# Dilation on one core: seven row sides as relu chains merged half by half into pair tiles, more clamped GpSimd pairs, other tile pitches and orders

## The chip, the core and the metric

The kernel runs on one core of a Trainium2 chip. Its time is device microseconds of that core. The core has TensorE (PE in the profile), VectorE (DVE), ScalarE (ACT), GpSimd (POOL) and SyncE (SP), which run their own instruction streams and meet at semaphores, 16 DMA engines, SBUF and PSUM as on-chip memory. GpSimd has no access to PSUM in this kernel: what lies in PSUM is touched by TensorE, ScalarE and VectorE alone.

## The reference, cut to what matters

`x` is (8, 32, 256, 256) in float32. It is normalised by groups of two channels, dilated with an 11 x 11 kernel for each channel and added to itself; then a second stage (projection, 3 x 3 depthwise convolution, batch norm, gelu, a small offset, bilinear resampling) is added too.

```python
def dilation(u, kernel, r):                       # r = 5, ks = 11, NEG = -1e30
    pad = jnp.pad(u, ((0, 0), (0, 0), (r, r), (r, r)), constant_values=NEG)
    kflat = kernel.reshape(C, ks * ks)
    def body(acc, idx):
        di = idx // ks
        dj = idx % ks
        sl = jax.lax.dynamic_slice(pad, (0, 0, di, dj), (Bn, C, H, W))
        return jnp.maximum(acc, sl - kflat[:, idx][None, :, None, None]), None
...
x = x + _L0_conv_ref(_gn(x), L0_conv_finsler_params)      # the dilation: 121 taps
x = x + _L1_conv_ref(_gn(x), ...)                         # convolution and resampling
```

## The kernel before, in words

The 256 planes lie in two groups of 128 partitions. A plane of 256 rows is taken in 16 windows of 16 rows (`WR`), each as two chunks of 8 rows (`CR`): 64 chunks, each 128 partitions x 2048 elements. `stats_and_tables` runs first, then `dilation` (L334 to L718), `convolution` and `resample`.

A window `u` has rows padded to `UC` = 266 elements; `dx` (`difference`, L179) holds u shifted by one minus u. The maximum of two neighbouring taps is base + relu(difference + gap), so a pair of taps costs one relu step, one addition of u and one maximum. There are three ways to do it:

- GpSimd pairs ("m", tiles `m`, 4 of them): ScalarE writes the relu (`pair_relu`, order letter r) or GpSimd itself a clamp of dx (`clamp`, L488, letter c, for pairs in `CLAMPED`); GpSimd adds u (`pair`, L496 and L500, letter t); VectorE takes the maximum into `acc_a` (L688, letter m).
- DMA pairs ("y", tiles `t`, 4): ScalarE writes the relu (letter x), GpSimd issues an accumulating DMA of u onto it (`add_u`, L471, letter i), VectorE merges it (letter y).
- Chains: one side of a kernel row, 5 or 6 taps, as repeated relu in PSUM, in two halves of 4 rows (`chain[0]`, `chain[1]`, letters 0 and 1): ScalarE a relu (`chain_step`, L609), TensorE adds dx or at last u (L559). VectorE merges the finished half into `acc_b` in SBUF (`merge_chain`, L662). The next chain's first relu waits for that (`chain_taken`).

Single taps (letter s) go from u into acc_a at once. `acc_a` lies in PSUM, each instruction on it waits for the one before (`a_done`). ScalarE starts acc_b from one tap (`start_b`, L576, letter b). At a chunk's end `join` takes the maximum of acc_a and acc_b (L695) and writes x1 = acc_a x rstd + u (L701), which SP stores; ScalarE squares x1 for the next statistics (letter u, L583), and the x1 of the next chunk waits for that. GpSimd also makes dx for the next window in pieces (L181, letter d).

Each engine's order inside a chunk is written out by hand in the strings `ACT_ORDER`, `PE_ORDER`, `DVE_ORDER`, `POOL_ORDER`. Counts per chunk, before: ScalarE 16 r, 16 x, 58 chain halves, b, u; VectorE 22 m, 16 y, 9 s, 12 chain merges, join, x1; GpSimd 22 t, 16 i, 6 c, 2 d; TensorE 58 half steps. A tile is free when VectorE has merged the pair that used it 4 pairs earlier (`a_free`, L404).

In `resample` (L1279 ff.) GpSimd makes three differences of y for each of 64 steps: dh (L1288, inputs one element apart), dv (L1291, inputs one row apart, y has pitch 257) and dd (L1295); VectorE does ten steps of 1024 elements with them.

## Time and profile before

| | |
|---|---|
| median of 3 runs | 10327.33 us (10327.08 to 10329.48) |
| profiled execution | 10330.04 us, span 10328.2 us |
| mean granted TensorE clock | 0.965 |
| VectorE, GpSimd, ScalarE, TensorE busy | 97%, 91%, 89%, 83% |
| t transfers (accumulating DMA) | 1024, 1059 KB each |

Busy shares are over the whole span and mix four stages. An instruction's duration on GpSimd reaches into the next one's; where an engine is never idle, the distance from start to start is what an instruction costs. The last part of the page, the chain that ended last, lies in the resampling alone and tells nothing of the dilation.

### The profile page before, as it was taken

The numbers are of one execution on the slowest core, as the hardware profiler recorded it, in microseconds if no ns is written. First come the engines' busy times: TensorE is split into PE (matmuls) and PEld (weight loads), VectorE is DVE, ScalarE is ACT, GpSimd is POOL, SyncE is SP. The second block draws the span as 40 slices with busy tenths as digits, with TensorE's granted clock in tenths as the row PEclk, the third lists the DMA queues.
The fourth block names the chain that finished last, engine by engine and source line by source line (L and its number), as shares of the span: only waits on it lengthen the run. The fifth ranks groups of instructions, "written<-read, shape, count | busy, mean of one in ns | idle before, by whom it ended". The sixth has DMA issues, their size and how long they took to land. (4 is left out here: it accounts for less than half of the span.)

```text
span 10328.2 us, 72612 instructions
## 1 busy us (share of the span) xinstructions
PE 8605.7 (83%) x18068; PEld 3331.9 (32%) x18068; DVE 9972.2 (97%) x5624; ACT 9184.8 (89%) x6857; POOL 9430.7 (91%) x3274
## 2 busy tenths in 40 slices
PE   2888888888888888888888888888888887997998
PEld 0333333333333333333333333333333332443333
DVE  8999999999999999999999999999999998999999
ACT  2999999999999999999999999999999997888776
POOL 2999999999999999999999999999999996777999
PEclk9999999999999999999999999999999998999999
DMA  8888878888888888788888888888888876444776
GB/s 320 152 155 154 153 153 156 159 158 157 157 157 158 157 158 160 150 158 160 157 157 157 156 156 156 159 157 159 157 158 157 157 139 132 173 189 178 264 278 253
DMA packets 442070, 1751.41 MB, mean 170 GB/s; under 512 B 23889, under 2 KB 130385, under 8 KB 392785
## 3 DMA queue, kind: packets, MB, share of 16 engines
q0 software_dynamic: 278528, 1110.51, 60.5%
q1 hardware_dynamic: 163152, 636.41, 16.3%
q8 instruction: 159, 2.61, 0.1%
q14 instruction: 231, 1.88, 0.1%
HBM read 391.58 MB, written 201.33 MB: 57 GB/s over the span
## 5 line engine op out<-in xcount | busy, mean ns | idle before, releaser
L559 PE MATMUL chain<-dx,mats 128*128 128x512 f32 x10240 | 5007.4, 635 | 922.9 <-ACT chain L609 921.4
L500 POOL TENSOR_TENSOR m<-m,u 128x2048 f32<-128x2048 f32 x1024 | 4817.0, 4891 | 25.0 <-ACT m L591 23.9
L688 DVE SCALAR_TENSOR_TENSOR acc_a<-m,kt,acc_a 128x2048 f32<-128x2048 f32 x1344 | 3162.9, 2353 | 74.0 <-POOL m L500 22.7
L559 PEld LDWEIGHTS chain<-dx,mats 128*128 128x128 f32 x10240 | 1923.6, 197 | 4006.5 <-ACT chain L609 2089.1
L609 ACT ACTIVATE chain<-chain,gap_r 128x1024 f32<-128x1024 f32 x2560 | 2699.5, 1089 | 233.7 <-PE chain L559 231.6
L688 DVE SCALAR_TENSOR_TENSOR acc_a<-t,kt,acc_a 128x2048 f32<-128x2048 f32 x1024 | 2412.0, 2355 | 34.2
L471 POOL DMA_DIRECT2D t<-u x1024 | 1680.5, 1752 | 396.8 <-ACT t L591 335.5
L496 POOL TENSOR_TENSOR m<-u,m 128x2048 f32<-128x2048 f32 x384 | 1914.8, 4986 | 0.0
L591 ACT ACTIVATE t<-dx,gap_l 128x2048 f32<-128x2048 f32 x768 | 1541.6, 2007 | 0.7 <-DVE acc_a L688 0.7
L559 PE MATMUL chain<-u,mats 128*128 128x512 f32 x3072 | 1456.0, 605 | 74.0 <-ACT chain L609 74.0
L688 DVE SCALAR_TENSOR_TENSOR acc_a<-u,kt,acc_a 128x2048 f32<-128x2048 f32 x576 | 1357.1, 2356 | 20.5
L591 ACT ACTIVATE m<-dx,gap_l 128x2048 f32<-128x2048 f32 x640 | 1282.3, 2004 | 22.6 <-DVE acc_a L688 22.6
L662 DVE SCALAR_TENSOR_TENSOR acc_b<-chain,kt,acc_b 128x1024 f32<-128x1024 f32 x768 | 966.6, 1279 | 69.6 <-PE chain L559 69.0
L559 PE MATMUL chain<-dx,neg_ident 128*128 128x512 f32 x1536 | 744.4, 621 | 330.9 <-ACT chain L609 313.6
L488 POOL TENSOR_SCALAR m<-dx,gap_l 128x2048 f32<-128x2048 f32 x384 | 989.4, 2577 | 12.8 <-DVE acc_a L688 12.6
L609 ACT ACTIVATE chain<-dx,gap_r 128x1024 f32<-128x1024 f32 x640 | 713.2, 1122 | 241.7 <-DVE acc_b L662 228.6
L559 PEld LDWEIGHTS chain<-u,mats 128*128 128x128 f32 x3072 | 547.2, 188 | 952.1 <-issue 557.7
L591 ACT ACTIVATE m<-dx,gap_r 128x2048 f32<-128x2048 f32 x384 | 766.8, 1997 | 0.0
L1052 DVE SCALAR_TENSOR_TENSOR hp<-o,par,hp 128x1024 f32<-128x1024 f32 x512 | 623.8, 1295 | 19.7 <-PE hp L863 19.6
L559 PEld LDWEIGHTS chain<-dx,neg_ident 128*128 128x128 f32 x1536 | 274.6, 192 | 800.7 <-ACT chain L609 520.8
L591 ACT ACTIVATE t<-dx,gap_r 128x2048 f32<-128x2048 f32 x256 | 516.7, 2018 | 13.9 <-PE chain L542 13.9
L964 POOL TENSOR_TENSOR tap_a<-tap_a,tap_b 128x2048 f32<-128x2048 f32 x64 | 291.7, 4558 | 236.8 <-ACT tap_b L927 225.8
(144 smaller groups left out, 7133.1 us busy)
## 6 DMA issues: line engine op xcount, KB each, us to landing
t<-u POOLq DMA_DIRECT2D x1024, 1059.0 KB, 8.8
u<-x_dram SPq DMA_DIRECT2D x32, 2688.0 KB, 30.8
xw<-x_scratch SPq DMA_DIRECT2D x62, 1152.0 KB, 7.3
xt<-x_dram SPq DMA_DIRECT2D x32, 2048.0 KB, 14.4
x_scratch<-x SPq DMA_DIRECT2D x64, 1024.0 KB, 10.6
h_scratch<-h SPq DMA_DIRECT2D x32, 2048.0 KB, 7.2
hw<-h_scratch SPq DMA_DIRECT2D x64, 1024.0 KB, 9.3
out_dram<-res SPq DMA_DIRECT2D x64, 1024.0 KB, 4.9
```

Source lines behind the costliest of these rows:

```text
L471: nc.gpsimd.dma_start(t[j % TP][:].rearrange("p r w -> p (r w)")[:, 0:RUN], u[s][:].rearrange("p r w -> p (r w)")[:, first:first + RUN], a ...
L488: nc.gpsimd.tensor_scalar(m[j % MP], dx[s][:, top:top + CR, lo:lo + W], high, low, ALU.min, ALU.max).then_inc(m_clamped, 1)
L496: nc.gpsimd.tensor_tensor(m[j % MP], rows, m[j % MP], ALU.add if outer > base else ALU.subtract).then_inc(m_ready, 1)
L500: nc.gpsimd.tensor_tensor(m[j % MP], m[j % MP], rows, ALU.add).then_inc(m_ready, 1)
L559: added = nc.tensor.matmul(chain[h][:, r:r + 2, :], weight, src[:, top:top + 2, dj:dj + W], start=False, stop=True, skip_group_check=True)
L591: return nc.scalar.activation(dst, dx[s][:, k * CR + di:k * CR + di + CR, lo:lo + W], ACT.Relu, bias=gap[:, g, col(di, base):col(di, base) ...
L609: nc.scalar.activation(chain[h][:], src, ACT.Relu, bias=gap[:, g, col(di, base):col(di, base) + 1], scale=scale).then_inc(chain_relu[h], 1)
L662: nc.vector.scalar_tensor_tensor(out=part, in0=chain[h][:], scalar=kt[:, g, base:base + 1], in1=part, op0=ALU.subtract, op1=ALU.max).then_ ...
L688: nc.vector.scalar_tensor_tensor(out=acc_a[:], in0=src, scalar=k_base, in1=acc_a[:], op0=ALU.subtract, op1=ALU.max).then_inc(a_done, 1)
L964: nc.gpsimd.tensor_tensor(tap_a[n % 2][:, rows, :], tap_a[n % 2][:, rows, :], tap_b[:, rows, :], ALU.add).then_inc(pool_adds, 1)
L1052: nc.vector.scalar_tensor_tensor(out=out, in0=o[n % 3][:, q * QR + ty:(q + 1) * QR + ty, tx:tx + W], scalar=par[:, COL_DW + t:COL_DW + t + 1],
```

## The change

- `CHAINS` gets a third entry (links) and a seventh chain: rows 0 (left) to 5 with 4 links (5 taps), row 6 with 5 links (6 taps). Before, six chains, the right ones with 5 links. The number of chain halves on ScalarE and TensorE stays 58.
- Pairs: 22 on GpSimd, 18 by DMA (16 before), 5 singles (9 and the one of acc_b before). Ten GpSimd pairs are clamped (6 before), so ScalarE has 12 r and 18 x.
- `acc_b`, `start_b` and the maximum in `join` are gone. A finished chain half is merged into a half of a pair tile that is ready but not yet merged (`chain_targets`: the second m or y tile that follows in `DVE_ORDER`), with the difference of the two kernel values (`k_gap`, 28 one-column subtractions ahead of the loop) as scalar. It waits for that tile (`tile_ready`), and the tile's own merge waits for the chain half (`chain_taken`).
- Five m and five t tiles instead of four each. The m tiles have pitch 266 instead of 260, and a pair's view starts at column (di * 266 + base + 2) % 4.
- y in `resample` has pitch 258 instead of 257.
- All four orders are new; VectorE's first instruction of a chunk is a single, the square moves to the end of ScalarE's chunk.
- The program is built with `dynamic_dma_scratch_size=4096`, the space for descriptors of the DMAs that GpSimd issues.

```diff
--- before.py
+++ after.py
@@ -48,20 +48,17 @@
-CHAINS = ((0, "left"), (1, "right"), (2, "right"), (3, "right"), (4, "right"), (5, "right"))
-NPOOL, NDMA = 16, 16
-CLAMPED = (1, 5, 9, 12, 16, 20)
-MP, TP = 4, 4
-ACT_ORDER = "x0x01r01xr10b1r01r01x01x01r01xr0u10r10x10x10x1r01r01r01x01x01x01r01r01x01r01rx010r10x10r10x1"
-PE_ORDER = "0011010101010101010101010101010101010101010101010101010101"
-DVE_ORDER = "m01mmymysss0m1myysymmy01mmsmyyms01msymsymm01ymymyysm0m1mymy"
-POOL_ORDER = "iitcitttcitittittcitdititcittiicttditittictitt"
+CHAINS = ((0, "left", 4), (1, "right", 4), (2, "right", 4), (3, "right", 4), (4, "right", 4), (5, "right", 4), (6, "right", 5))
+NPOOL, NDMA = 22, 18
+CLAMPED = (0, 2, 3, 4, 7, 8, 11, 12, 13, 15)
+MP, TP = 5, 5
+ACT_ORDER = "x0x10r10x10x1x0r10r10x10x1r01x01x01x01r0101x01r1x0x1x01x01r01x0r10r10r1010rx01x01r01u0101"
+PE_ORDER = "0101010101010101010101010101101010101010101010100101010101"
+DVE_ORDER = "smy0m1ymymms01myymym01mymymy1y0mmmyms10ymysym10mmymmyym01sy"
+POOL_ORDER = "cdcdcititticitttciitictitcittcitictitticitittttiitit"
@@ -74,20 +71,35 @@
     pairs, singles = [], []
+    sides = {di: (side, links) for di, side, links in CHAINS}
     for di in range(KS):
-        side = dict(CHAINS).get(di)
+        side, links = sides.get(di, (None, 0))
...
             pairs += [(di, 1, 0), (di, 3, 2)]
-            singles += [(di, 4)]
+            if links == 4:
+                pairs += [(di, 5, 4)]
+            else:
+                singles += [(di, 4)]
...
             singles += [(di, 10)]
-    while len(pairs) > NPOOL + len(CLAMPED) + NDMA:
+    while len(pairs) > NPOOL + NDMA:
...
+def chain_targets():
+    targets = {}
+    order = list(numbered(DVE_ORDER))
+    for place, (kind, ch) in enumerate(order):
+        if kind in "01":
+            tiles = [x for x in order[place + 1:] if x[0] in "my"]
+            targets[int(kind), ch] = tiles[:2][-1]
+    return targets
@@ -336,8 +348,9 @@
     D_TURNS = POOL_ORDER.count("d")
-    pool_pairs, dma_pairs, (init_b, *singles) = dilation_taps()
-    NPAIR = NPOOL + len(CLAMPED)
+    pool_pairs, dma_pairs, singles = dilation_taps()
+    targets = chain_targets()
+    NPAIR = NPOOL
@@ -352,8 +365,8 @@
     chain_steps = []
-    for ch, (di, side) in enumerate(CHAINS):
-        bases = range(1, 5) if side == "left" else range(9, 4, -1)
+    for ch, (di, side, links) in enumerate(CHAINS):
+        bases = range(1, 1 + links) if side == "left" else range(9, 9 - links, -1)
@@ -371,9 +384,9 @@
-        m = [sb(f"m{s}", [P, CR, W + 4])[:, :, 0:W] for s in range(MP)]
+        m_tiles = [sb(f"m{s}", [P, CR, UC]) for s in range(MP)]
         t = [sb(f"t{s}", [P, CR, UC]) for s in range(TP)]
-        acc_b = sb("acc_b", [P, CR, W])
+        k_gap = sb("k_gap", [P, GROUPS, 2 * NCHAIN])
@@ -392,11 +405,23 @@
         chain_taken = [sem(f"chain_taken{h}") for h in range(2)]
-        b_started = sem("b_started")
+        k_gap_ready = sem("k_gap_ready")
         a_done = sem("a_done")
-        merged = sem("merged")
...
+        def m_tile(j):
+            di, base, outer = pool_pairs[j]
+            first = (di * UC + base + 2) % 4
+            return m_tiles[j % MP][:, :, first:first + W]
+        def tile_of(kind, j):
+            return m_tile(j) if kind == "m" else t[j % TP][:, :, 0:W]
+        def tile_col(kind, j):
+            di, base, outer = pool_pairs[j] if kind == "m" else dma_pairs[j]
+            return col(di, outer if kind == "m" and j in CLAMPED else base)
@@ -485,7 +510,7 @@
                     passed(pool, pool_turns)
-                    nc.gpsimd.tensor_scalar(m[j % MP], dx[s][:, top:top + CR, lo:lo + W], high, low,
+                    nc.gpsimd.tensor_scalar(m_tile(j), dx[s][:, top:top + CR, lo:lo + W], high, low,
@@ -493,11 +518,11 @@
                         pool.wait_ge(m_clamped, c * len(CLAMPED) + (CLAMPED.index(j) + 1))
-                        nc.gpsimd.tensor_tensor(m[j % MP], rows, m[j % MP],
+                        nc.gpsimd.tensor_tensor(m_tile(j), rows, m_tile(j),
...
                         pool.wait_ge(m_begun, c * NRELU + (relu_pairs.index(j) + 1))
-                        nc.gpsimd.tensor_tensor(m[j % MP], m[j % MP], rows, ALU.add).then_inc(m_ready, 1)
+                        nc.gpsimd.tensor_tensor(m_tile(j), m_tile(j), rows, ALU.add).then_inc(m_ready, 1)
@@ -545,7 +570,7 @@
                     ch, step, base = chain_steps[i]
-                    di, side = CHAINS[ch]
+                    di, side, _ = CHAINS[ch]
@@ -569,13 +594,6 @@
             def _(act):
-                def start_b(c, s, k):
-                    di, dj = init_b
-                    act.wait_ge(merged, at(c, 1, 0))
-                    nc.scalar.activation(acc_b[:], u[s][:, k * CR + di:k * CR + di + CR, dj:dj + W], ACT.Identity,
-                                         bias=nkt[:, g, col(di, dj):col(di, dj) + 1]).then_inc(b_started, 1)
@@ -594,7 +612,7 @@
                     ch, step, base = chain_steps[i]
-                    di, side = CHAINS[ch]
+                    di, side, _ = CHAINS[ch]
@@ -626,14 +644,12 @@
                                         act.wait_ge(a_done, a_free(c, "m", relu_pairs[j], NPAIR, MP))
-                                        pair_relu(s, k, pool_pairs[relu_pairs[j]], m[relu_pairs[j] % MP]) \
+                                        pair_relu(s, k, pool_pairs[relu_pairs[j]], m_tile(relu_pairs[j])) \
...
                                         pair_relu(s, k, dma_pairs[j], t[j % TP][:, :, 0:W]).then_inc(t_ready, 1)
-                                    elif kind == "b":
-                                        start_b(c, s, k)
@@ -644,59 +660,61 @@
                 nc.vector.memset(x1[:], 0.0).then_inc(pads_set, 1)
+                for g in range(GROUPS):
+                    for (h, ch), tile in targets.items():
+                        last = col(CHAINS[ch][0], chain_steps[last_step[ch]][2])
+                        other = tile_col(*tile)
+                        nc.vector.tensor_tensor(k_gap[:, g, 2 * ch + h:2 * ch + h + 1], kt[:, g, last:last + 1],
+                                                kt[:, g, other:other + 1], ALU.subtract).then_inc(k_gap_ready, 1)
+                dve.wait_ge(k_gap_ready, GROUPS * 2 * NCHAIN)
                 dve.sem_inc(a_done, NA)
-                dve.sem_inc(merged, 1)
...
-                def merge_chain(c, h, ch):
-                    di, side = CHAINS[ch]
-                    base = col(di, chain_steps[last_step[ch]][2])
-                    part = acc_b[:, h * HR:(h + 1) * HR, :]
-                    dve.wait_ge(chain_added[h], c * NSTEP + (last_step[ch] + 1))
-                    dve.wait_ge(chain_taken[h], at(c, NCHAIN, ch))
-                    if ch == 0:
-                        dve.wait_ge(b_started, c + 1)
-                    nc.vector.scalar_tensor_tensor(out=part, in0=chain[h][:], scalar=kt[:, g, base:base + 1], in1=part,
-                                                   op0=ALU.subtract, op1=ALU.max).then_inc(chain_taken[h], 1)
-                def merge(c, s, k, kind, j):
+                def tile_ready(c, kind, j):
...
                         dve.wait_ge(m_ready, c * NPAIR + (j + 1))
-                        di, base, outer = pool_pairs[j]
-                        if j in CLAMPED:
-                            base = outer
-                        src = m[j % MP]
-                    elif kind == "y":
+                    else:
                         dve.wait_ge(t_added[j % TP], c * (len(range(j % TP, NDMA, TP)) * 16) + (j // TP + 1) * 16)
-                        passed(dve, dve_turns)
-                        di, base, outer = dma_pairs[j]
-                        src = t[j % TP][:, :, 0:W]
+                def merge_chain(c, h, ch):
+                    tile = targets[h, ch]
+                    part = tile_of(*tile)[:, h * HR:(h + 1) * HR, :]
+                    dve.wait_ge(chain_added[h], c * NSTEP + (last_step[ch] + 1))
+                    tile_ready(c, *tile)
+                    if ch > 0 and targets[h, ch - 1] == tile:
+                        dve.wait_ge(chain_taken[h], at(c, NCHAIN, ch))
+                    nc.vector.scalar_tensor_tensor(out=part, in0=chain[h][:],
+                                                   scalar=k_gap[:, g, 2 * ch + h:2 * ch + h + 1], in1=part,
+                                                   op0=ALU.subtract, op1=ALU.max).then_inc(chain_taken[h], 1)
+                def merge(c, s, k, kind, j):
+                    if kind == "s":
+                        di, base = singles[j]
+                        src, at_col = u[s][:, k * CR + di:k * CR + di + CR, base:base + W], col(di, base)
                     else:
-                        di, base = singles[j]
-                        src = u[s][:, k * CR + di:k * CR + di + CR, base:base + W]
-                    k_base = kt[:, g, col(di, base):col(di, base) + 1]
+                        tile_ready(c, kind, j)
+                        src, at_col = tile_of(kind, j), tile_col(kind, j)
+                        for h in range(2):
+                            taken = [ch for (half, ch), tile in targets.items() if half == h and tile == (kind, j)]
+                            if taken:
+                                dve.wait_ge(chain_taken[h], at(c, NCHAIN, max(taken) + 1))
+                    k_base = kt[:, g, at_col:at_col + 1]
...
                         dve.wait_ge(joined, at(c, 1, 0))
-                        passed(dve, dve_turns)
...
-                def join(c, s, k):
+                def finish(c, s, k):
+                    dve.wait_ge(x1_squared, c + 1)
                     dve.wait_ge(a_done, at(c, NA, NA))
-                    for h in range(2):
-                        dve.wait_ge(chain_taken[h], at(c, NCHAIN, NCHAIN))
-                    nc.vector.tensor_tensor(acc_a[:], acc_a[:], acc_b[:], ALU.max).then_inc(merged, 1)
-                    dve.wait_ge(x1_squared, c + 1)
-                    dve.wait_ge(merged, at(c, 1, 1))
-                    passed(dve, dve_turns)
@@ -715,7 +733,7 @@
                                         merge(c, s, k, kind, j)
-                                join(c, s, k)
+                                finish(c, s, k)
@@ -1074,7 +1092,7 @@
         xw = [sb(f"xw{s}", [P, VR + 1, W]) for s in range(XS)]
-        y = [sb(f"y{s}", [P, VR + 1, W + 1]) for s in range(2)]
+        y = [sb(f"y{s}", [P, VR + 1, W + 2])[:, :, 0:W + 1] for s in range(2)]
@@ -1440,7 +1458,8 @@
     }
-    nc = bacc.Bacc("TRN2", target_bir_lowering=False, num_devices=1)
+    nc = bacc.Bacc("TRN2", target_bir_lowering=False, num_devices=1,
+                   dynamic_dma_scratch_size=4096)
...
     build(nc, *args, out)

```

## Rows read from the trace of the kernel before

**Rows 1.** The profile page, part 1: busy us of each engine and its share.
```profile
PE 8605.7 (83%) x18068; PEld 3331.9 (32%) x18068; DVE 9972.2 (97%) x5624; ACT 9184.8 (89%) x6857; POOL 9430.7 (91%) x3274
```

**Rows 2.** The trace by line, L685, the first VectorE instruction of each of 64 chunks.
```profile
L685 DVE TENSOR_SCALAR acc_a<-m,kt x64: 2353/2354/2356, 212.8 to 8588.3; 128x2048 f32<-128x2048 f32 x64
```

**Rows 3.** The timeline of VectorE, one chunk's end: start us, us, instruction, idle before.
```profile
3001.92 2.36 DVE L688 SCALAR_TENSOR_TENSOR acc_a<-m,kt,acc_a 128x2048 f32<-128x2048 f32 x1
3004.31 2.36 DVE L688 SCALAR_TENSOR_TENSOR acc_a<-t,kt,acc_a 128x2048 f32<-128x2048 f32 x1
3006.86 2.30 DVE L695 TENSOR_TENSOR acc_a<-acc_a,acc_b 128x2048 f32<-128x2048 f32 x1 [0.20 <-DVE acc_a L688]
3009.40 2.35 DVE L701 SCALAR_TENSOR_TENSOR x<-acc_a,small,u 128x2048 f32<-128x2048 f32 x1 [0.24 <-DVE acc_a L695]
3011.90 2.35 DVE L685 TENSOR_SCALAR acc_a<-m,kt 128x2048 f32<-128x2048 f32 x1
3014.17 2.47 DVE L662 SCALAR_TENSOR_TENSOR acc_b<-chain,kt,acc_b 128x1024 f32<-128x1024 f32 x2
3016.55 2.35 DVE L688 SCALAR_TENSOR_TENSOR acc_a<-m,kt,acc_a 128x2048 f32<-128x2048 f32 x1
```

**Rows 4.** The timeline of GpSimd in the dilation.
```profile
3006.34 3.35 POOL L488 TENSOR_SCALAR m<-dx,gap_l 128x2048 f32<-128x2048 f32 x1
3008.26 2.60 POOL L471 DMA_DIRECT2D t<-u  x1
...
3029.49 2.33 POOL L471 DMA_DIRECT2D t<-u  x1
3030.28 5.76 POOL L496 TENSOR_TENSOR m<-u,m 128x2048 f32<-128x2048 f32 x1
3034.43 5.75 POOL L500 TENSOR_TENSOR m<-m,u 128x2048 f32<-128x2048 f32 x1
3038.55 2.81 POOL L471 DMA_DIRECT2D t<-u  x1
...
3055.88 3.06 POOL L181 TENSOR_TENSOR dx<-u 128x1060 f32<-128x1060 f32 x1
3057.77 2.32 POOL L471 DMA_DIRECT2D t<-u  x1
```

**Rows 5.** The timeline of ScalarE in the dilation.
```profile
3025.51 2.00 ACT L591 ACTIVATE t<-dx,gap_l 128x2048 f32<-128x2048 f32 x1
3027.40 2.09 ACT L609 ACTIVATE chain<-chain,gap_r 128x1024 f32<-128x1024 f32 x2
3029.39 2.02 ACT L591 ACTIVATE m<-dx,gap_r 128x2048 f32<-128x2048 f32 x1
```

**Rows 6.** DMA view, 1000 to 8000 us: queue's packets, MB, share; issue's KB, us to landing.
```profile
q0 software_dynamic: 229216, 913.88, 73.5%
q1 hardware_dynamic: 102096, 183.01, 7.4%
...
t<-u POOLq DMA_DIRECT2D x844, 1059.0 KB, 8.8
```

**Rows 7.** The timeline of GpSimd in the convolution.
```profile
8976.06 4.55 POOL L969 TENSOR_TENSOR h<-h,tap_a 128x2048 f32<-128x2048 f32 x1
8980.57 4.55 POOL L964 TENSOR_TENSOR tap_a<-tap_a,tap_b 128x2048 f32<-128x2048 f32 x1
```

**Rows 8.** The timeline of GpSimd in the resampling.
```profile
9851.82 4.56 POOL L1291 TENSOR_TENSOR dv<-y 128x2048 f32<-128x2048 f32 x1
9856.45 3.60 POOL L1295 TENSOR_TENSOR dd<-dv 128x2048 f32<-128x2048 f32 x1
9860.01 3.60 POOL L1288 TENSOR_TENSOR dh<-y 128x2048 f32<-128x2048 f32 x1
9863.57 4.55 POOL L1291 TENSOR_TENSOR dv<-y 128x2048 f32<-128x2048 f32 x1
```

**Rows 9.** The timeline of VectorE in the resampling.
```profile
9860.18 1.23 DVE L1371 SCALAR_TENSOR_TENSOR tx<-tx,dd 128x1024 f32<-128x1024 f32 x1 [0.18 <-POOL dd L1295]
```

6 lines of the change are left out of this document (3 added, 3 removed).

## The prediction

> **What bounds the kernel now.** I read the page's busy times first [rows 1]: VectorE is busy for 97% of the span, GpSimd for 91%, ScalarE for 89%, so none of them can be called the bound from that line. The dilation has to be read for itself. Its chunk loop starts 64 times, from 212.8 to 8588.3 us [rows 2]: 8375.5 / 63 = 132.94 us a chunk, 64 chunks are 8508 us, 82% of the span. For what an instruction costs I take the distance to the next start on its engine, not its duration, because on GpSimd the durations overlap: a pair addition is shown with 5.75 us, yet the next instruction starts 4.12 us later [rows 4].
>
> VectorE, by its timeline [rows 3]: a maximum into acc_a 2.39 us when another follows, 2.27 when a chain merge follows, 2.55 at the end of the chunk, a chain merge 1.19 (two in 2.38), the join 2.54, the x1 step 2.50. The order of before has 47 instructions into acc_a, 8 of them ahead of a group of chain merges: 38 x 2.39 + 8 x 2.27 + 2.55 + 12 x 1.19 + 2.54 + 2.50 = 130.9 us. That leaves 132.94 - 130.9 = 2.0 us of stalls. GpSimd [rows 4]: 22 pairs x 4.14 (the rows show 4.15 and 4.12), 6 clamps x 1.92, 16 issues x 0.79, two pieces of dx x 1.89: 91.1 + 11.5 + 12.6 + 3.8 = 119.0 us. ScalarE [rows 5]: 32 pair steps x 1.89, 29 x 1.99 for two chain halves, the square and acc_b at least another two at 1.89: 60.5 + 57.7 + 3.8 = 122.0 us. The DMA engines [rows 6]: 73.5% + 7.4% of 132.94 = 97.7 + 9.8 = 107.5 us, or 6.11 us for each of the 16 t transfers. So VectorE is the bound of the dilation, by some 9 us over ScalarE, 12 over GpSimd and 23 over DMA. The resampling stage is the other place touched. There GpSimd runs without a gap, 11.75 us a step (3.56 dh, 4.63 dv with its handover, 3.56 dd) [rows 8], and VectorE waits only 0.18 us of it, for dd [rows 9].
>
> **The change, part by part, in one chunk.** Of 121 taps, seven chains now take 36, 40 pairs take 80, 5 are singles.
>
> VectorE: two y more and four s less (init_b counted out) make 45 instructions into acc_a, the join is gone, and there are 14 chain merges in 9 groups: 35 x 2.39 + 9 x 2.27 + 2.55 + 14 x 1.19 + 2.50 = 125.8 us, 5.1 less. A chain merge into a tile has the shape of one into acc_b, one operand in PSUM and one in SBUF, so I leave it at 1.19. What it adds is a wait: it needs the tile up to two tiles ahead of its own turn, and everything later on VectorE is queued behind it, as are ScalarE's next chain (chain_taken) and the buffers (a_done). Ahead of it only a tile's lateness counts, up to two instructions (4.8 us) earlier than now; the fifth m and t tile give one more buffer for it. A merge directly behind its own chain merge occurs nowhere, there is always an instruction between, so I put no stall there. The 28 one-column subtractions for k_gap stand once ahead of the loop: under 0.1 us each, 2.5 us in all, nothing hides them.
>
> ScalarE: four r less, two x more, no acc_b: 3 x 1.89 less, 116.3 us. The square moves from the first half of the chunk to its end; four chain halves (4 us) are behind it, and x1 is only written again at the next chunk end, so nothing.
>
> DMA: 18 x 6.11 + 9.8 = 119.8 us. This was 23 us clear of VectorE and is now 6 us clear.
>
> GpSimd: four clamps and two issues more, 7.7 + 1.6 us; at the old price of a pair 91.1 + 19.2 + 14.2 + 3.8 = 128.3 us. That is over VectorE's 125.8, so the price of a pair decides. The m tiles get the row pitch of u (266 instead of 260 elements) and a first column that puts every row two elements (8 bytes) off the row of u in its 16 bytes. What do rows say of that? Three forms of one size of addition stand in this trace: dh and dd, whose inputs are one element apart in one tile, 3.56 us; dv and the two additions of the convolution, 4.51 (start to start of h and tap_a [rows 7]; dv took 4.55) [rows 8]; the pairs 4.14. h and tap_a have their rows at the same place in 16 bytes; dv's inputs are 257 elements apart, one element off. In the pairs of before, pitches 260 and 266 differ by 6, so the offset alternates by two elements from row to row: half of the rows of an even base lie as in h, half two elements off. If only the offset within 16 bytes counts, 4.14 is the mean of 4.51 and the price of the other half, which is 2 x 4.14 - 4.51 = 3.77 us. The lower end is 3.56, the upper 4.14 for a price that hangs on something else, and 4.51 if the like pitches put all rows into the slow case. I take 3.77, as the one value that accounts for 4.14 and 4.51 together. GpSimd is then at 82.9 + 19.2 + 14.2 + 3.8 = 120.1 us.
>
> A page speaks against this. The Trainium skill, GPSIMD Engine Reference, section 3 (Performance versus the Vector engine), holds that an addition with two inputs costs about 2.5 to 2.6 cycles an element because both reads go through one port, and gives 4497 ns for 2048 elements; by that there is nothing to gain. This trace agrees for h and tap_a (4.51) and disagrees for dh and dd, the same size at 3.56 to 3.60. By the page all pairs would go at 4.5; what that would make is rival C, worked out there from rows.
>
> So the floor falls from 130.9 to 125.8 us. Stalls were 2.0 us with three engines well clear; now GpSimd and DMA stand at 95% of the floor and ScalarE at 93%. One place is tight: the new chunk begins on GpSimd with clamp, piece, clamp, piece, clamp (9.5 us) ahead of its first issue, and a transfer lands 8.8 us after its issue [rows 6]. The clamp can start only when m20 is merged, 17 us before VectorE ends the chunk (y15, y16, m21, two merges, s4, y17, x1), so the first transfer lands 1.5 us into the next chunk and the second, 6.1 us later, at 7.6, where the first chain merge wants it at 7.05. It just fits, with the x1 store in the same queues. I take 2.8 us of stalls (the old 2.0 and this), 128.6 us a chunk: 64 x (132.94 - 128.6) = 278 us saved. In the resampling y gets pitch 258: dv's inputs are two elements off, the same 3.77; GpSimd needs 11.0 us a step, VectorE's 11.57 becomes the bound, 0.18 x 62 = 11 us. Sum: 278 + 11 - 2.5 = 286.5 us. The profiled execution took 10330.0 us (span 10328.2), the median of the runs is 10327.3, 2.7 lower; from that median 10041 us.
>
> **The rivals.** (A) As told, 10041; by stalls of 1.7 to 4 us, 9971 to 10118.
> (B) The pair stays at 4.14 us. For it: two pairs of different base cost 4.15 and 4.12 [rows 4], as they would if the offset didn't matter. GpSimd is the bound at 128.3; with 2 us of stalls 130.3, with 4 at the chunk's turn, where it waits for m20, 132.3. 64 x (132.94 - 130.3) = 169, and nothing in the resampling: 10161, up to 10290.
> (C) Slower: like pitches put each row into the case of h and dv. 22 x 4.51 + 37.2 = 136.4 us on GpSimd, with 1 us of stalls 137.4: 64 x 4.46 + 2.5 = 288 us more, 10615. It decides from a pair price of (132.9 - 37.2 - 1) / 22 = 4.30 us on; below that the kernel is faster. Against it: only the rows in h's position should cost that, and none is there.
> (D) Pairs at 3.77, but the chunk is held by t transfers: the queue is empty for about 5 us at each chunk's turn (last landing 10 us before the end, where the last chains merge into y17; first bytes of the next 8.8 - 6.1 = 2.7 us behind its issue, 4.6 before the end), 119.8 + 5 = 125 us, and the x1 store and window loads push y0 and y1 late; 5 us of stalls, 131 us. 64 x 1.94 = 124 us and 11 from the resampling, less 2.5, 10195.
> (E) The smaller descriptor space (4096) makes GpSimd wait at an issue. A transfer has 272 packets, and no row bounds what a full space costs: nothing, or up to a landing (8.8 us) at some issues. One wait of 8.8 a chunk on GpSimd would give 128.6 + stalls, near B.
>
> **Chances.** A 0.57, B 0.18, C 0.09, D 0.12, E and others 0.04. The predicted time is A's. The range takes A, two thirds of B and most of D: 9950 to 10230 us. What a measurement of this kernel can tell from no change is about 0.2%, 20 us. Faster by more than that: A, nearly all of B and D, half of E, 0.87; within it 0.03; slower 0.10 (C and the rest).
>
> **What would show it.** Start to start of a pair addition on GpSimd: 3.77 (A, D), 4.14 (B), 4.5 (C). dv near 3.8 with VectorE without a gap in the resampling, step 11.6 us. The chunk at 128.6 us; VectorE's waits at a chain merge for a DMA or GpSimd small in A, large at the first y of the chunk in D; the DMA share in the dilation 93% where it was 81%. An issue that costs over 0.8 us would be E. The forecast falls if the pair price doesn't move, or if four resources within 7% of each other stall more than 4 us a chunk.

## The result and the profile after

The changed kernel takes 11291.88 us (median of 4 runs, 11281.61 to 11297.98), the kernel before 10327.33: ratio 1.0934, 95% interval 1.0917 to 1.0951. It is 9.3% slower, where 2.8% faster was forecast. The profiled execution has a span of 11279.8 us.

Part 1 of the page, busy us and share of the span of each engine, to be read beside [rows 1]:

```profile
PE 8588.7 (76%) x18068; PEld 3360.2 (30%) x18068; DVE 9689.9 (86%) x5589; ACT 8875.1 (79%) x6665; POOL 9524.3 (84%) x3658
```

The busy times of VectorE and ScalarE fell by 282 and 310 us, near what the count of instructions said, and GpSimd's rose by only 94. Every share fell: the engines wait. Where they do so, the first VectorE instruction of the 64 chunks tells, as in [rows 2]:

```profile
L709 DVE TENSOR_SCALAR acc_a<-u,kt x64: 2353/2353/2355, 195.6 to 9556.1; 128x2048 f32<-128x2048 f32 x64
```

(9556.1 - 195.6) / 63 = 148.6 us a chunk, where it was 132.94 and 128.6 was forecast. 64 x 15.6 = 998 us more; the loop starts 17 us earlier (195.6 for 212.8, because the first instruction is now a single that needs no tile), and the resampling takes 22 us less. Together these give 959 us, against 952 between the two profiled spans: the loss is in the dilation. The mean granted TensorE clock fell too, from 0.965 to 0.928, but it went to the same 0.928 when the kernel before was only made to wait (experiment 1), so it goes with the waiting.

The waits of VectorE between 1000 and 8000 us (line waited for, us in total, times, longest us):

```profile
DVE acc_a L712 <- POOL m L521: 636.5, 24, 28.2
DVE t L689 <- DMA t<-u: 174.3, 69, 5.3
DVE m L689 <- POOL m L521: 122.7, 89, 3.3
DVE t L689 <- PE chain L584: 55.6, 87, 2.5
DVE acc_a L712 <- DMA t<-u: 45.1, 67, 1.1
DVE m L689 <- PE chain L584: 43.4, 38, 2.8
```

7000 us are 47.1 chunks, so the rows add up to 1077.6 / 47.1 = 22.9 us a chunk, and 148.6 - 22.9 = 125.7: the forecast's floor for VectorE of 125.8 is there, and the error is all in the waits. Five rows share 9.4 us a chunk. One row has 13.5 us, in only 24 places of 26.5 us each: once in each window of two chunks. It names an addition on GpSimd, but that is not the cause, since it was late itself. The timeline of GpSimd at such a place (start us, us, instruction, idle before):

```profile
3147.23 1.97 POOL L513 TENSOR_SCALAR m<-dx,gap_l 128x2048 f32<-128x2048 f32 x1
3179.26 1.95 POOL L193 TENSOR_TENSOR dx<-u 128x1060 f32<-128x1060 f32 x1 [30.07 <-DMA u<-x_dram]
...
3186.98 1.17 POOL L496 DMA_DIRECT2D t<-u  x1
3187.77 4.24 POOL L521 TENSOR_TENSOR m<-u,m 128x2048 f32<-128x2048 f32 x1
```

VectorE at the same place:

```profile
3161.56 2.35 DVE L719 SCALAR_TENSOR_TENSOR x<-acc_a,small,u 128x2048 f32<-128x2048 f32 x1
...
3163.96 2.35 DVE L709 TENSOR_SCALAR acc_a<-u,kt 128x2048 f32<-128x2048 f32 x1
3192.14 2.36 DVE L712 SCALAR_TENSOR_TENSOR acc_a<-m,kt,acc_a 128x2048 f32<-128x2048 f32 x1 [25.83 <-POOL m L521]
```

And SyncE's queue:

```profile
3164.74 1.80 SPq L188 DMA_DIRECT2D u<-x_dram  x2
```

Read together: the piece of dx in the second place of GpSimd's order reads the next window's u. That buffer is the one that the x1 step at 3161.56 still reads, so SyncE issues the load only at 3164.74, behind that step, and it lands at 3179.26, 14.5 us later. GpSimd is 16.7 us ahead of VectorE here (3147.23 for 3163.96). It stands at the piece for those 16.7 us and the load's 14.5, with all its clamps, additions and issues queued behind: 30 us, once in a window. The view of line 193 says so over the whole run (sat idle until, us, times; 172 us of it are the very first wait of the kernel, as before, so the other 28 are 30.8 us each):

```profile
L193 POOL TENSOR_TENSOR dx<-u x134: 1060/1952/1956, 172.9 to 9280.0; 128x1060 f32<-128x1060 f32 x132, 128x530 f32<-128x530 f32 x2
...
  DMA u<-x_dram: 1033.8, 29
```

In the kernel before the same instruction waited for no load but the very first. Its SyncE queue and its GpSimd at a window's end:

```profile
3144.74 2.67 SPq L176 DMA_DIRECT2D u<-x_dram  x2
...
3189.05 2.37 POOL L181 TENSOR_TENSOR dx<-u 128x1060 f32<-128x1060 f32 x1
```

There the piece stood in the 21st place, 44.3 us behind the issue of the load.

What was forecast of the parts is there. GpSimd in the dilation, to be set beside [rows 4]:

```profile
3095.46 7.32 POOL L521 TENSOR_TENSOR m<-u,m 128x2048 f32<-128x2048 f32 x1
3099.23 7.28 POOL L525 TENSOR_TENSOR m<-m,u 128x2048 f32<-128x2048 f32 x1
3102.97 4.70 POOL L496 DMA_DIRECT2D t<-u  x1
3103.76 5.93 POOL L513 TENSOR_SCALAR m<-dx,gap_l 128x2048 f32<-128x2048 f32 x1
3105.69 5.18 POOL L496 DMA_DIRECT2D t<-u  x1
```

A pair addition takes 3.77 us to the next start (3095.46 to 3099.23), an issue 0.79, a clamp 1.93. The resampling [rows 8]:

```profile
10861.84 3.60 POOL L1306 TENSOR_TENSOR dh<-y 128x2048 f32<-128x2048 f32 x1 [0.48 <-ACT y L1244]
10865.40 3.82 POOL L1309 TENSOR_TENSOR dv<-y 128x2048 f32<-128x2048 f32 x1
10869.30 3.60 POOL L1313 TENSOR_TENSOR dd<-dv 128x2048 f32<-128x2048 f32 x1
```

dv takes 3.82 us where it took 4.55, GpSimd now idles 0.48 us a step and VectorE runs without a gap. The 64 dv start from 10526.8 to 11244.9 us: 11.40 us a step for 11.75, 22 us in all. The DMA view from 1000 to 8000 us, beside [rows 6]:

```profile
q0 software_dynamic: 229105, 913.48, 73.9%
...
t<-u POOLq DMA_DIRECT2D x844, 1059.0 KB, 12.3
```

73.9% of 148.6 us is 109.8 us for 18 transfers, 6.1 us each as before, but each lands 12.3 us behind its issue, where it was 8.8.

### The profile page after: what moved, and what is told of

Same layout as the page of the kernel before. It is cut to its first block and busy times, and to the rows that moved or that the text cites. A ratio compares the mean times of both kernels' runs of the same rounds, so it can differ in the third digit from the quotient of the medians.

```text
span 11279.8 us, 73600 instructions
## 1 busy us (share of the span) xinstructions
PE 8588.7 (76%) x18068; PEld 3360.2 (30%) x18068; DVE 9689.9 (86%) x5589; ACT 8875.1 (79%) x6665; POOL 9524.3 (84%) x3658
## 5 line engine op out<-in xcount | busy, mean ns | idle before, releaser
L525 POOL TENSOR_TENSOR m<-m,u 128x2048 f32<-128x2048 f32 x768 | 3853.0, 5691 | 143.2 <-ACT m L609 143.2
L496 POOL DMA_DIRECT2D t<-u x1152 | 3454.8, 3278 | 180.6 <-ACT t L609 178.7
L521 POOL TENSOR_TENSOR m<-u,m 128x2048 f32<-128x2048 f32 x640 | 3483.8, 6239 | 0.0
L712 DVE SCALAR_TENSOR_TENSOR acc_a<-t,kt,acc_a 128x2048 f32<-128x2048 f32 x1152 | 2712.5, 2355 | 93.2 <-DMA t<-u 60.4
L513 POOL TENSOR_SCALAR m<-dx,gap_l 128x2048 f32<-128x2048 f32 x640 | 2588.9, 4045 | 12.9 <-DVEq L670 9.7
L609 ACT ACTIVATE t<-dx,gap_l 128x2048 f32<-128x2048 f32 x960 | 1920.2, 2000 | 1.4 <-DVE acc_a L712 1.4
L689 DVE SCALAR_TENSOR_TENSOR t<-chain,k_gap,t 128x1024 f32<-128x1024 f32 x448 | 568.1, 1281 | 314.1 <-DMA t<-u 232.2
L609 ACT ACTIVATE m<-dx,gap_l 128x2048 f32<-128x2048 f32 x384 | 770.2, 2006 | 0.0
L689 DVE SCALAR_TENSOR_TENSOR m<-chain,k_gap,m 128x1024 f32<-128x1024 f32 x448 | 564.1, 1280 | 224.2 <-POOL m L521 163.0
L712 DVE SCALAR_TENSOR_TENSOR acc_a<-u,kt,acc_a 128x2048 f32<-128x2048 f32 x256 | 602.5, 2354 | 6.9
## 6 DMA issues: line engine op xcount, KB each, us to landing
t<-u POOLq DMA_DIRECT2D x1152, 1059.0 KB, 12.3
xt<-x_dram SPq DMA_DIRECT2D x32, 2048.0 KB, 14.4
```

Source lines behind the costliest of these rows:

```text
L496: nc.gpsimd.dma_start(t[j % TP][:].rearrange("p r w -> p (r w)")[:, 0:RUN], u[s][:].rearrange("p r w -> p (r w)")[:, first:first + RUN], a ...
L513: nc.gpsimd.tensor_scalar(m_tile(j), dx[s][:, top:top + CR, lo:lo + W], high, low, ALU.min, ALU.max).then_inc(m_clamped, 1)
L521: nc.gpsimd.tensor_tensor(m_tile(j), rows, m_tile(j), ALU.add if outer > base else ALU.subtract).then_inc(m_ready, 1)
L525: nc.gpsimd.tensor_tensor(m_tile(j), m_tile(j), rows, ALU.add).then_inc(m_ready, 1)
L609: return nc.scalar.activation(dst, dx[s][:, k * CR + di:k * CR + di + CR, lo:lo + W], ACT.Relu, bias=gap[:, g, col(di, base):col(di, base) ...
L689: nc.vector.scalar_tensor_tensor(out=part, in0=chain[h][:], scalar=k_gap[:, g, 2 * ch + h:2 * ch + h + 1], in1=part, op0=ALU.subtract, op1 ...
```

## The experiments

Ratios are to the kernel before on the same chip, with 95% intervals. The chunk is worked out as above, from the first and last start of the instruction that opens acc_a; a wait a chunk is the row's sum between 1000 and 8000 us over the chunks in it.

| run | median us | ratio | chunk us |
|---|---|---|---|
| after | 11291.88 | 1.0934 [1.0917, 1.0951] | 148.6 |
| before, d early | 11299.18 | 1.0933 [1.0915, 1.0951] | 148.3 |
| after, d late | 10667.33 | 1.0327 [1.0310, 1.0344] | 138.8 |
| before, m pitch | 10298.36 | 0.9967 [0.9954, 0.9979] | 132.4 |
| d late, old m pitch | 10974.22 | 1.0620 [1.0602, 1.0637] | 143.6 |
| d late, half transfers | 10297.58 | 0.9968 [0.9953, 0.9983] | 132.9 |
| d late, half additions | 10332.83 | 1.0005 [0.9995, 1.0015] | 133.5 |
| before, merged into tiles | 11006.16 | 1.0655 [1.0637, 1.0672] | 143.5 |
| d late, acc_b back, 4 m tiles | 11001.50 | 1.0654 [1.0636, 1.0672] | 143.8 |
| d late, acc_b back, 5 m tiles | 10438.65 | 1.0100 [1.0083, 1.0117] | 135.3 |
| d late, nearest tile | 10454.21 | 1.0104 [1.0084, 1.0124] | 135.4 |
| nearest tile, half transfers | 10185.13 | 0.9861 [0.9844, 0.9877] | 131.2 |
| before, pitches, five tiles | 11293.37 | 1.0925 [1.0907, 1.0944] | 148.5 |
| before, pitches, four tiles | 10283.35 | 0.9957 [0.9943, 0.9970] | 132.4 |
| before, pitches, even ring | 10275.52 | 0.9951 [0.9937, 0.9965] | 132.4 |

### 1. The place of the two pieces of dx, from both sides

In the kernel after, only the order of GpSimd is changed, so that the two pieces stand in the 23rd and 37th place (52 and 86 us behind the first clamp in a chunk of its trace):

```diff
-POOL_ORDER = "cdcdcititticitttciitictitcittcitictitticitittttiitit"
+POOL_ORDER = "cccititticitttciitictidtcittcitictitdticitittttiitit"
```

> The changed kernel with one edit: the two dx pieces (d) in POOL_ORDER stand 48 and 81 us into GpSimd's chunk, as in the kernel before, and not second and fourth. Theory 1: the loss is GpSimd's wait for the next window's u at the first d (1034 us in the trace of the changed kernel, 32 us in the first chunk of each window); without it the chunk goes to 128 to 130 us and the kernel to 10050 to 10150 us. Rival: the second chunk of a window, which has no such wait, took 133.6 us in the changed kernel, with VectorE waiting at chain merges for t and m tiles; if these waits belong to the new structure and not to the recovery from the long wait, the chunk stays near 133 and the kernel near 10340 us. A third: the piece is not the cause (load itself late), then over 11000 us.

And in the kernel before only the pieces are moved, to the third and fifth place:

```diff
-POOL_ORDER = "iitcitttcitittittcitdititcittiicttditittictitt"
+POOL_ORDER = "iidtdcitttcitittittcitititcittiicttitittictitt"
```

> The kernel before with one edit: the two dx pieces moved to places 3 and 5 of GpSimd's chunk (from places 21 and 35). Theory 1: GpSimd leads VectorE by 11 us at a chunk's start, u's buffer is free only at VectorE's window end and the load lands 15 to 31 us later, so GpSimd waits 25 to 40 us once a window; some 5 us a chunk of slack on GpSimd give a part back, VectorE loses 20 to 32 us a window, the kernel takes 10950 to 11300 us. If the early piece is harmless in itself: 10320 to 10400 us.

Measured: the kernel after gains 9.8 us a chunk, 625 us of the 965 lost. It lies above what the first two theories had given and below the third, so the early piece is the largest part of the loss but not all of it. The kernel before loses 15.3 us a chunk, as much as the whole change, by two letters moved. Its view of line 181 (sat idle until, us, times):

```profile
  DMA u<-x_dram: 883.2, 29
```

The cause is shown from both sides. With d late line 193 still waits for the load: 247.8 us at 22 places, of which 172 are again the very first wait, so 75 us at 21 places, 3.6 us each and 1.2 us a chunk on GpSimd. The first chunk of a window is still the longer one (140.5 us against 137.0). What is left is 138.8 us where 128.6 was forecast. VectorE's waits in the run with d late:

```profile
DVE m L689 <- POOL m L521: 209.4, 94, 3.4
DVE acc_a L712 <- DMA t<-u: 194.2, 119, 3.9
DVE m L689 <- PE chain L584: 132.9, 123, 8.9
DVE t L689 <- DMA t<-u: 48.7, 51, 1.7
DVE t L689 <- PE chain L584: 26.6, 32, 1.4
DVE acc_a L712 <- POOL m L525: 8.5, 6, 2.2
```

620 / 50.4 chunks = 12.3 us a chunk: a chain half that waits for its m tile, transfers, and chains. These rows gave 9.4 us beside the long wait in the kernel after, so a part of what the long wait had covered came out when it went. The next runs take these one by one.

### 2. The price of the pair addition

The row pitch and first column of the m tiles alone, put into the kernel before:

```diff
-        m = [sb(f"m{s}", [P, CR, W + 4])[:, :, 0:W] for s in range(MP)]
+        m_tiles = [sb(f"m{s}", [P, CR, UC]) for s in range(MP)]
...
+            first = (di * UC + base + 2) % 4
+            return m_tiles[j % MP][:, :, first:first + W]
```

> The kernel before with the m tiles' pitch and first column of the change alone (rows of m two elements off the rows of u). The pair addition on GpSimd goes from 4.14 to 3.77 us start to start, as it does in the changed kernel. GpSimd is not the bound here, VectorE's stalls (2.0 us a chunk) can only shrink: 10230 to 10330 us, likeliest 10290. If the price came from the new order or the neighbours and not from the place of the rows, pairs stay at 4.14 and the time at 10327.

And taken out of the kernel after with d late (pitch W + 4, first = 0):

> e1_after_d_late with the m tiles of before: pitch 260, first column 0. The pairs go back to 4.14 us, GpSimd has 128.3 us of work a chunk. Theory 1: GpSimd becomes the bound, 130 to 133 us a chunk, 2 to 4 us more than e1_after_d_late, so 130 to 260 us more than it. If something else holds e1_after_d_late (DMA, waits for tiles), the same time as it within 60 us.

Measured: 0.33% faster in the kernel before (132.4 us a chunk, 0.5 less). In the other, GpSimd's timeline shows the old price, 3020.24 to 24.37 = 4.13 us:

```profile
3020.24 5.27 POOL L521 TENSOR_TENSOR m<-u,m 128x2048 f32<-128x2048 f32 x1
3024.37 2.33 POOL L496 DMA_DIRECT2D t<-u  x1
```

and the chunk is 4.8 us longer (143.6 against 138.8; 2 to 4 had been expected), where 22 x 0.37 = 8.1 us of work came back. So the pitch works as its price says, is worth 4.8 us where GpSimd is near the bound and 0.5 where it is 12 us clear of it. Rivals B and C are excluded.

### 3. The transfers, and GpSimd's work

The eighteen accumulating transfers on four of the eight rows:

```diff
-                    nc.gpsimd.dma_start(t[j % TP][:].rearrange("p r w -> p (r w)")[:, 0:RUN],
-                                        u[s][:].rearrange("p r w -> p (r w)")[:, first:first + RUN],
+                    nc.gpsimd.dma_start(t[j % TP][:].rearrange("p r w -> p (r w)")[:, 0:RUN // 2],
+                                        u[s][:].rearrange("p r w -> p (r w)")[:, first:first + RUN // 2],
```

> e1_after_d_late with each accumulating t transfer on the first four of its eight rows only (half of the addition of u to the t tiles is left out). The DMA work falls from some 120 to 65 us a chunk, everything else stays. Theory DMA: the backlog of transfers (12 to 21 us from issue to landing in e1 where 8 is the least) holds VectorE; then the chunk falls from 138.7 to 129 to 131 us, kernel 10060 to 10180. Theory coupling (a chain merge now waits for a pair tile, ScalarE's next chain for the merge, the relus and issues behind it for ScalarE): the loop stays, 134 to 138 us, 10380 to 10620.

Measured: 132.9 us, 5.9 less, between the ranges of the two theories. VectorE's waits for transfers (194.2 and 48.7 us above) are gone; its waits for an m tile are not:

```profile
DVE m L689 <- POOL m L521: 261.8, 106, 3.1
DVE t L689 <- PE chain L584: 50.3, 100, 1.3
```

Why 120 us of transfers hold a chunk of 139 is seen at its turn, in the run with d late and whole transfers. The first VectorE instruction of one chunk starts at 3394.62. This is the stretch from 15 to 6 us before it (us, busy times of PE, PEld, DVE, ACT and POOL, granted clock, DMA share, GB/s):

```profile
3379.62:3388.62 9.00, 7.83 (x19) 3.17 (x18) 8.86 (x6) 6.89 (x6) 6.50 (x5) 1.00 0.14 24
```

In the 15 us on either side the DMA share is full. Over 29 such turns between 2000 and 6000 us the mean share of this stretch is 0.20, some 7 us in which the DMA engines have nothing to do; in the kernel before it is 0.63, some 3 us.

The other way round, GpSimd's additions on four of eight rows, the transfers whole:

```diff
-                        nc.gpsimd.tensor_tensor(m_tile(j), m_tile(j), rows, ALU.add).then_inc(m_ready, 1)
+                        nc.gpsimd.tensor_tensor(m_tile(j)[:, 0:HR, :], m_tile(j)[:, 0:HR, :], rows[:, 0:HR, :], ALU.add).then_inc(m_ready, 1)
```

> e1_after_d_late with GpSimd's 22 pair additions on the first four rows only (half of that addition is left out): some 39 us a chunk less on GpSimd, issues and tiles come earlier, DMA and VectorE unchanged. If GpSimd's load (120 us of work in order, not buffers or DMA) holds the chunk: 128 to 131 us, 10060 to 10180. Theory DMA: at or over 133. Theory coupling: the m part of the waits goes, the t part stays: 132 to 136 us, 10300 to 10500.

Measured: 133.5 us on the mean, but of two kinds: the second chunk of each window takes 126.5 us, VectorE's floor with 0.6 us of waits, the first 140.7. The reason is in the last of these waits of GpSimd from 1000 to 8000 us:

```profile
POOL t L496 <- ACT t L609: 923.2, 387, 7.2
POOL m L525 <- ACT m L609: 671.6, 262, 5.1
POOL dx L193 <- DMA u<-x_dram: 453.8, 26, 18.8
```

With less work it gets further ahead of VectorE and stands at the window's load again, although the piece is still in its late place. This confirms the floor of 125.8, and shows that an engine made faster brought a wait back (17.5 us at each of 26 places) that it had all but escaped by being slow. It doesn't give GpSimd's share of the loss by itself.

### 4. The chain half that is merged into a tile

In the kernel before, acc_b, its first instruction on ScalarE and the join are taken out and the chain halves go into the second tile behind, all orders else as they were (ScalarE's without b, VectorE's with one more s):

```diff
-                    part = acc_b[:, h * HR:(h + 1) * HR, :]
+                    tile = targets[h, ch]
+                    part = tile_of(*tile)[:, h * HR:(h + 1) * HR, :]
...
+                    tile_ready(c, *tile)
```

> The kernel before with one part of the change alone: no acc_b and no join, the chain halves go into the second pair tile that follows, its tap a tenth single at the end of the chunk (so VectorE's own work is 130.8 us a chunk as before, 48 x 2.39 instead of 47 and the join). Six chains, 22 and 16 pairs, four m and four t tiles, all pitches and orders as before. Theory coupling: VectorE's merges wait for tiles, ScalarE's chains for the merges: the chunk rises by 3 to 8 us over 132.9, kernel 10500 to 10850. Theory DMA: nothing is added to DMA or GpSimd, ScalarE has 1.9 us less: 10290 to 10380.

Measured: 143.5 us a chunk, 10.6 more than before (3 to 8 had been expected), with pair and transfer counts, tiles and pitches unchanged. VectorE's waits:

```profile
DVE m L689 <- POOL m L521: 386.9, 147, 6.3
DVE m L689 <- POOL m L525: 226.1, 49, 4.9
```

613 / 48.8 chunks = 12.6 us, where all waits were 2.2 before. Merging into a tile is dear in an order where the tile comes just in time. The same test on the other side, the kernel after with d late and acc_b back, first with four m tiles because of memory, then with five:

```diff
-MP, TP = 5, 5
+MP, TP = 4, 5
...
-                    tile = targets[h, ch]
-                    part = tile_of(*tile)[:, h * HR:(h + 1) * HR, :]
+                    part = acc_b[:, h * HR:(h + 1) * HR, :]
```

> e1_after_d_late with acc_b, start_b and the join put back (seven chains merge into acc_b again, one single less; VectorE's work 126.0 us a chunk as against 125.8; ScalarE 1.9 more), four m tiles instead of five to make room. Theory coupling: the waits of merges for tiles go, 130 to 133 us a chunk, 10140 to 10340 us. Theory DMA: it stays at 136 to 140, 10500 to 10750; a fourth reading, that the fifth m tile mattered, would look the same and show as waits of GpSimd's clamps for acc_a.

> e7_late_acc_b with five m tiles instead of four: e1_after_d_late with acc_b and the join in place of the merges into tiles, and no other difference on purpose. In e7 ScalarE waited 11.5 us a chunk for a free m tile, so e7 did not tell the coupling. Theory coupling: chain merges no longer wait for tiles, 129 to 134 us a chunk as against 138.7 in e1, kernel 10060 to 10380. If the coupling costs nothing in the new structure: 10620 to 10720, as e1.

Measured: 143.8 us with four tiles, 135.3 with five. The first is no test of the merge: these orders were laid out for five tiles, and one tile less costs 8.5 us. The second is: 3.5 us less than with the merge into tiles, at nearly the same work for VectorE (the join of 2.54 us is back, one single of 2.39 us is gone). It is still above the 129 to 134 us that had been expected, and its largest wait is for transfers, 244.7 us in the same 7000. Third way, the half goes into the next tile instead of the second next, so that VectorE asks for no tile before its turn:

```diff
-            targets[int(kind), ch] = tiles[:2][-1]
+            targets[int(kind), ch] = tiles[0]
```

> e1_after_d_late with one edit: a chain half is merged into the next pair tile in VectorE's order, not the second one, so each merge asks for a tile one tile earlier in the ring that is due anyway, 2.4 us later than before. Theory coupling: waits of merges for tiles shrink; 1 to 5 us a chunk less than e1, kernel 10350 to 10600. Against it: a tile's own merge can now follow its chain merge at once, 0.2 us each time, 14 times, which alone would make it 180 us slower: 10700 to 10850.

Measured: 135.4 us, 3.4 less. Its waits:

```profile
DVE t L689 <- DMA t<-u: 151.7, 72, 4.5
DVE acc_a L712 <- DMA t<-u: 117.9, 75, 3.7
...
DVE acc_a L712 <- DVE m L689: 29.9, 156, 0.2
...
DVE m L689 <- POOL m L521: 7.8, 9, 2.4
```

The wait for GpSimd's tile fell from 209.4 to 7.8 us, and the DMA share at the turn is 0.59 where it was 0.20. The new order has a price of its own: four times a chunk (156 times for an m tile, 52 for a t tile) the next instruction waits 0.2 us for the merge itself, and VectorE's time outside its waits for other engines rises from 126.4 to 128.0 us a chunk (28 chunks between 2000 and 6000 us in either run). What stays is the transfers, 5.2 us a chunk, and some 1.7 us for chains.

### 5. All three at once

The nearest tile and half transfers together, d late:

> The kernel after with the d pieces late in the chunk, the chain half merged into the nearest tile, and the eighteen accumulating transfers on four of the eight rows (the lower four rows of the t sums lack the second reading; that part of the computation is left out). Theory that the late d, the merge's tile and the transfers' backlog are the three causes of the loss and nearly independent: 135.1 us a chunk of the nearest-tile run less the 5.9 that the half transfers saved gives 129.2 us, with VectorE's work of 127.5 as the floor: 10454.21 - 5.9 x 64 = 10077 us (10040 to 10120), which is the forecast's 128.6 us. Rival, that they overlap (with fewer transfers GpSimd gets further ahead and waits for the window's load again, or the tile's release decides): 131 to 133 us, 10190 to 10320 us.

Measured: 131.2 us, 2.0 more than expected. The expectation started from 135.1 us where the whole loop of the nearest-tile run gives 135.4; from that, the sum of the single effects is 129.5 and the overlap 1.7 us. The chunk is just inside the rival's range, the kernel's time 5 us below it. VectorE's waits:

```profile
DVE m L689 <- PE chain L584: 104.7, 207, 1.9
DVE acc_a L712 <- DVE m L689: 30.8, 161, 0.2
DVE t L689 <- PE chain L584: 26.7, 35, 3.0
DVE acc_a L712 <- POOL m L525: 20.1, 19, 2.8
```

The view of line 193 has no wait for a load but the first, so the rival's reason (GpSimd gets ahead again) is wrong. The largest wait left is another one: chains that come late from ScalarE and TensorE, 131.4 / 53.4 = 2.5 us a chunk, where the run with d late had 159.5 / 50.4 = 3.2. Of the 5.4 us over the counted floor of 125.8, all waits for other engines are 3.0; the rest is VectorE itself, whose time outside them is 128 us as in the nearest-tile run. That only four engines so near to each other make these 3 us is argued, not shown: no run took the chains' waits away.

### 6. Five tiles in the kernel before

The kernel before with everything of the change that leaves its orders and its merges alone: both pitches, five m and five t tiles, the smaller descriptor space.

```diff
-MP, TP = 4, 4
+MP, TP = 5, 5
...
-        y = [sb(f"y{s}", [P, VR + 1, W + 1]) for s in range(2)]
+        y = [sb(f"y{s}", [P, VR + 1, W + 2])[:, :, 0:W + 1] for s in range(2)]
...
+                   dynamic_dma_scratch_size=4096)
```

> The kernel before with the parts of the change that should only help: m tiles in the new place (e3), y with pitch 258, five m and five t tiles, descriptor space 4096; orders, chains, acc_b as before. e3 gave 10298 (132.3 us a chunk, floor 130.8). The resampling step goes from 11.75 to 11.41 us as in the changed kernel: 21 us less. If more tiles take stalls away, up to another 90 us: 10200 to 10280 us. If the smaller descriptor space makes issues wait, over 10300 and issues of over 0.8 us start to start.

Measured: 148.5 us a chunk, 16 more than with the m pitch alone, and 11293 us where 10200 to 10280 had been expected. ScalarE's first wait between 1000 and 8000 us, and VectorE at a chunk's turn:

```profile
ACT t L596 <- DVE acc_a L693: 693.6, 47, 15.2
```

```profile
3036.51 2.35 DVE L690 TENSOR_SCALAR acc_a<-m,kt 128x2048 f32<-128x2048 f32 x1 [9.95 <-POOL m L505]
```

Once a chunk (47 times in 47.1 chunks) ScalarE waits some 15 us for VectorE to release a t tile. Tiles are dealt by number modulo their count, afresh in each chunk. Sixteen t steps modulo four leave the ring at its start, so the first of a chunk takes the tile of the fourth last. Modulo five leaves one over: the first of a chunk takes the tile of the very last, y15, which VectorE reads as the last tile of the chunk. One tile more took the distance at the turn from four tiles to one. Two runs separate this from the pitches and the descriptor space: the same kernel with four tiles again, and with t at four but the 22 pairs of m on five tiles in even blocks (5, 5, 4, 4, 4; the expectation gives the blocks wrongly), so that no pair comes nearer than four tiles over the turn.

```diff
+def ring(uses, tiles):
+    blocks = -(-uses // tiles)
+    short = blocks * tiles - uses
+    return [x for b in range(blocks) for x in range(tiles - (b >= blocks - short))]
...
-            return m_tiles[j % MP][:, :, first:first + W]
+            return m_tiles[MSLOT[j]][:, :, first:first + W]
```

> The run before + pitches + five tiles with four m and four t tiles again: the kernel before with the m pitch and first column, the y pitch and the descriptor space of 4096. The whole output is computed. Theory of the ring at the turn: the tile count alone made that run slow, so here the chunk takes 132.3 us as in the run with the m pitch alone, and the resampling gives 21 us more than that run: 10298 - 21 = 10277 us (10265 to 10290). Rival, that the descriptor space makes issues wait: 10350 us or more. Rival, that the pitches together take another way: 11200 us.

> Kernel before with the m pitch and first column, the y pitch and the smaller descriptor space of after, as in the run before + pitches + five tiles; but the m ring has five tiles used in blocks of 5, 4, 4, 3 (sixteen pairs), so that the last clamps of a chunk and the first of the next are four tiles apart, and t has four tiles. The whole output is computed. Theory of the ring at the chunk's turn (sixteen pairs modulo five tiles leave the first pair of a chunk only one tile behind the last of the one before, and ScalarE waits 15.2 us a chunk for it): that wait goes, the chunk takes 130.8 to 132.3 us where five tiles modulo took 148.5, and with resampling at some 11.4 us a step (-21 us in all) the kernel takes 10220 to 10285 us. Rival, that the pitches or the descriptor space cost the 16 us a chunk of that run: 11200 to 11300 us.

Measured: 132.4 us a chunk in both, 10283 (four m tiles) and 10276 us (five in the even ring). With t on four tiles ScalarE's wait for a t tile is gone from both traces. Together with the wait itself, which names the t tile, this makes the uses modulo the tiles of t the cause; t on five tiles in an even ring, and four t tiles beside five m tiles dealt by modulo, were not run. Pitches and descriptor space cost nothing together, which excludes rival E here; the fifth m tile in an even ring brings nothing that can be told from four (the intervals overlap). Both beat both kernels of this case: 0.4 to 0.5% below the kernel before, of which 0.3 are the m pitch; the rest fits the resampling, where dv takes 3.82 us in both runs.

In the kernel after, 18 uses on five t tiles leave a distance of three at the turn, and 22 on five m tiles one of two; before it was four and two. Another ring was not tried there, but its trace has the waits: ScalarE and GpSimd together wait 1.6 us for a tile's release (line 712) between 1000 and 8000 us, and ScalarE 54.9 us, 1.1 us a chunk, with d late. So the ring is no large part of this loss.

## Why the prediction was wrong, point by point

**VectorE's floor: right.** 125.8 us were counted; 148.6 less the waits is 125.7, and the undisturbed chunk of the run with half additions takes 126.5 with 0.6 us of waits. A merge into a tile costs 1.19 us. The 28 subtractions ahead of the loop take 1.8 us (192.8 to 194.6) where 2.5 were put down.

**Pair price: right.** 3.77 us, start to start, taken from the mean of two cases [rows 4, 7]; 4.13 with the old pitch. By the sentence of the Trainium skill quoted in the prediction (GPSIMD Engine Reference, section 3) it would have been 4.5; the measurement decides against it. The number came out, but the model behind it is not whole. The prediction let the offset within 16 bytes alone decide, yet dv before and dh both had inputs one element off and took 4.55 and 3.56 us. And it reckoned 4.14 as a mean for pairs of even base, whose rows lie 0 and 2 elements off in turn; 13 of the 22 pairs have an odd base, with rows 1 and 3 off, and cost the same (4.12 to 4.16 us for the clamped pairs, three of either kind). So the right number stood on weaker ground than the working says.

**The failed step: "clamp, piece, clamp, piece, clamp (9.5 us) ahead of its first issue".** The pieces were costed as 1.89 us of work each, unchanged, and their move was put at nothing. The wait that the first one carries, for the window's load, wasn't moved with it in the sum. Both halves of its price stood in the working or in the trace: GpSimd begins a chunk "17 us before VectorE ends" it, and the load is issued by SyncE behind VectorE's last step. In the kernel before the load takes 13.5 to 31.7 us and the piece comes 44.3 us behind its issue. Moved ahead of all, it costs the lead and the load, by the trace of the kernel after 16.7 + 14.5 us less the 1.9 of the first clamp, each window: (31.2 - 1.9) / 2 = 14.7 us a chunk on GpSimd, of which 13.5 reach VectorE. Moving it back gave 9.8 us, moving it in the kernel before cost 15.3. Without that step and with the rest as it was, the forecast would still have been wrong:

**Stalls of 2.8 us: mis-sized.** Without the wait for the window they are 12.3 us a chunk. Three things are in them. First the merge into the second next tile. The prediction saw the wait and priced it at nothing as long as the tile isn't more than two instructions late; measured, it is 3.4 us (nearest tile) to 3.5 (acc_b back), and 10.6 in the orders of before. Second the transfers: 119.8 us of DMA work beside 125.8 was called "6 us clear", and it isn't clear, because the DMA engines have some 7 us of nothing to do at the chunk's turn; 119.8 + 7 is over 125.8. With half transfers 5.9 us go (4.2 together with the nearest tile). This was rival D, with its 5 us of stalls sized about right, though the waits lie 10 to 70 us into the chunk (with d late, 4.8 us in all) and not at its first y; as it adds to the others and doesn't replace them, a chance of 0.12 for it alone was the wrong form. Third the chains, 3.2 us with d late and 2.5 when the others are gone. The closest test, with the early piece, the merge's tile and the transfers' backlog away, gives 131.2 us for the forecast's 128.6.

**Resampling: the right way, half the size.** 22 us instead of 11: VectorE's own step is 11.40 us and not 11.57.

**Rivals.** B and C fell with the price, D is there as one part of several, E didn't happen (an issue is 0.79 us). The slower side had been looked for in the price of an instruction alone, where it came from the order. The 2.0 us that the sum of rows left open in the kernel before were carried over into the new order nearly as they stood; two edits to that kernel, the early piece and the merge into tiles, raise its chunk by 15.3 and 10.6 us, so they were small because of its order and its acc_b.

## What to carry to other kernels

An instruction that is moved takes its waits with it: ahead of its price ask what releases it, at what time, and how far its engine runs ahead of that one, for here a wait at the head of GpSimd's order cost its lead plus the load's latency. A merge into a buffer makes its consumer need that buffer earlier, and with two resources within 5% of the bound their small waits add up instead of hiding behind each other. When a ring of buffers restarts with each round, the uses modulo the buffers say how deep it is at the turn; one buffer more can make it shallower.
